# Reworking the projections and the first key pass of a two-layer gated cross-attention kernel

## The reference

```python
x = x + tanh(g_xattn[0]) * L0_xattn(layernorm(x), ctx, Wq, bq, Wkv, bkv, Wp, bp)
x = x + tanh(g_ffn[0])   * L0_ffn(layernorm(x), ...)          # mixture of low-rank experts
x = x + tanh(g_xattn[1]) * L1_xattn(layernorm(x), ctx, wq, bq, wkv, bkv, wp, bp)
x = x + tanh(g_ffn[1])   * L1_ffn(layernorm(x), ...)          # ternary weights

# L0_xattn: one softmax of every token over the keys of all 8 sequences
q = fq_sym((x @ Wq + bq) / 4, per token and head)             # round(q / s) * s, s = max|q| / 127
k = fq_sym(cond @ Wkv[:, :256] + bkv[:256], per key and head)
v = fq_sym(cond @ Wkv[:, 256:] + bkv[256:], per column, over all keys)
attn = fq_unsigned(softmax(q k^T), per row)                   # steps of max / 255
out = (attn @ v) @ Wp + bp

# L1_xattn: within a sequence
out = qdq(softmax(q k^T / 4) @ v) @ qdq(wp)^T + bp            # qdq: round(x / s) * s per row, s = max|x| / 127
```

## Time and profile before

| | us |
|---|---|
| median of three executions | 6873.82 |
| profiled execution | 6872.02 |
| its span | 6870.2 |
| first_keys, from its first POOL memset to the next stage | 122.16 to 552.89 |
| first_values | 552.89 to 703.03 |
| first_attention up to the first matmul | 703.03 to 732.82 |
| first row maxima, then the main loop | 732.82 to 5011.6 |
| project(0) | 5016.03 to 5081.78 |
| feed-forward, second queries and keys, second attention | to 6448 |
| project(1) | 6449.45 to 6550.16 |
| gated feed-forward | to 6870.2 |

### The profile page before, as it was taken

The page is one execution under the profiler, slowest core; times in us unless marked ns, Lnnn a source line. Parts: engine busy times, 40 slices in busy tenths (PEclk is TensorE's granted clock), DMA queues, the critical chain, the costliest instruction groups (busy, mean ns, idle before and its releaser), DMA issues. The chain is left out here.

```text
span 6870.2 us, 178673 instructions
## 1 busy us (share of the span) xinstructions
PE 5802.4 (84%) x63503; PEld 2380.6 (35%) x63510; DVE 5704.3 (83%) x8942; ACT 4387.7 (64%) x4251; POOL 3741.3 (54%) x3973
## 2 busy tenths in 40 slices
PE   2771699999999999999999999999949487999523
PEld 2331133333333333333333333333334353544311
DVE  5886699999999999999999999999943556777655
ACT  0330089988989889989889989989912013666301
POOL 2331078888888888878888888888810001000000
PEclk7995599999999999999999999999969697999756
DMA  1442211011011011011011011011020078877500
GB/s 57 112 108 94 46 22 18 9 26 19 9 26 19 9 26 18 10 26 18 10 26 18 11 25 19 11 25 19 10 48 0 19 303 181 116 112 114 85 28 9
DMA packets 182852, 319.86 MB, mean 47 GB/s; under 512 B 97220, under 2 KB 143813, under 8 KB 176803
## 3 DMA queue, kind: packets, MB, share of 16 engines
q1 hardware_dynamic: 181944, 307.93, 21.0%
HBM read 196.59 MB, written 113.33 MB: 45 GB/s over the span
## 5 line engine op out<-in xcount | busy, mean ns | idle before, releaser
L1024 DVE TENSOR_REDUCE a_mx<-PS 128x1 f32<-128x512 f32 x6620 | 4073.2, 688 | 230.1 <-PE PS L908 226.5
L995 ACT ACTIVATE a_e<-PS,a_sk 126x1024 f32<-126x1024 f32 x3264 | 3634.0, 1114 | 458.2 <-PE PS L893 109.6
L771 POOL TENSOR_SCALAR a_p<-a_e 126x1024 f16<-126x1024 f32 x3264 | 3418.1, 1047 | 641.0 <-ACT a_e L995 588.5
L908 PE MATMUL PS<-a_K,a_Q 48*128 48x512 bf16 (+1 forms) x6884 | 2109.8, 383 | 49.9 <-DMA a_K<-d_inv 49.9
L893 PE MATMUL PS<-a_Q,a_K 54*126 54x512 bf16 x6528 | 2113.3, 404 | 26.6 <-issue 17.4
L935 PE MATMUL PS<-a_e,a_sel 126*32 126x256 f32 x26112 | 1994.7, 382 | 0.0
L893 PEld LDWEIGHTS PS<-a_Q,a_K 54*126 54x126 bf16 x6528 | 615.4, 131 | 1377.3 <-issue 1319.6
L931 PE MATMUL PS<-a_p,a_V 128*32 128x256 f16 x13056 | 960.1, 284 | 14.1 <-ACT a_og L976 10.0
L931 PEld LDWEIGHTS PS<-a_p,a_V 128*32 128x32 f16 x13056 | 336.8, 93 | 1251.6 <-POOL a_p L771 1059.0
L935 PEld LDWEIGHTS PS<-a_e,a_sel 126*32 126x32 f32 x26112 | 756.1, 110 | 8.9 <-issue 2.4
L1891 DVE TENSOR_REDUCE b_mx<-PS 128x1 f32<-128x512 f32 x803 | 504.8, 685 | 188.4 <-PE PS L1775 188.4
(11 more groups left out here) (300 smaller groups left out, 3363.9 us busy)
## 6 DMA issues: line engine op xcount, KB each, us to landing
b_K<-d_k SPq DMA_DIRECT2D x210, 200.1 KB, 6.1
a_K<-d_k SPq DMA_DIRECT2D x102, 400.2 KB
d_v<-v1v SPq DMA_DIRECT2D x9, 3328.0 KB, 10.3
b_V<-d_v SPq DMA_DIRECT2D x36, 832.0 KB, 12.1
d_k<-k_T SPq DMA_DIRECT2D x400, 63.0 KB, 1.7
d_k<-k1p SPq DMA_DIRECT2D x54, 400.2 KB, 7.7
a_V<-d_v SPq DMA_DIRECT2D x68, 204.0 KB, 2.8
d_v<-vq SPq DMA_DIRECT2D x17, 803.2 KB
```

The costliest lines, as they stand in the source:

```text
L771: g.tensor_scalar(p[0:rows, kk % RE, :], e[0:rows, kk % RE, :], 1.0, SHIFT, ALU.mult, ALU.add).then_inc(rounded, 1)
L908: last = pe.matmul(self.PS[:, M_BANK + j % sh.SLOTS, c0:c0 + wd], Qb[M_ROWS, ii % 4, t * P:(t + 1) * P], Kb[M_ROWS, (ii // NC) % 2, k0:k0 ...
L995: a.activation(e[0:r, kk % RE, :], self.PS[0:r, e_bank(i, s):e_bank(i, s) + 2, :], ACT.Exp, scale=skb[0:r, hb, s:s + 1]).then_inc(exp_done, 1)
L1024: v.tensor_reduce(mx[:, col:col + 1], bank, AX.X, ALU.max).then_inc(max_done, 1)
```

## The change

- **first_keys.** Keys and values of both tiles now lie in a bank each. The bias is added by PE: DVE splits it once into three bf16 parts (rows 0, 32 and 64 of `bp`), and a 96-row bf16 matmul with a matrix of ones in those rows (`pick`) adds it to each of the four PSUM regions. DVE reads the keys straight from PSUM; ACT makes the values (`v_raw`) and their magnitudes (`v_abs`), and casts the high and middle bf16 parts. DVE keeps a running maximum of the magnitudes (`v_top`). DVE works on group g and the rest of group g - 1 in turn; PE turns group g - 2; ACT evacuates group g - 3 in two copies of 1008 columns and one of 252. SP stores a group with three DMAs.
- **first_values.** The maximum over partitions is taken by two PE transposes, a reduction of 2 x 126, two diagonal matrices and one matmul with ones. Scaling goes in two halves; each head's store and column sums are released as the head is rounded.
- **first_attention.** The three key parts for the row maxima are loaded first, in five pieces of keys, and PE waits for each piece where it needs it. POOL clears the 34 semaphores of the earlier stages ahead of its memsets.
- **project.** Sums are loaded as 16 rows, turned on PE, and their reciprocals taken from PSUM; no trip through DRAM. Layer 0: ACT spreads the reciprocals over each head's 16 columns, PE turns them, DVE applies them and the value scales in one instruction a half. Layer 1: the output is turned before the reciprocals are applied, bank by bank; rows and weight go as integers in bf16 through PE, the scales are applied to the product, the bias (times the gate) is added to x early. In both, DVE takes the product bank by bank while PE goes on.

```diff
@@ first_keys @@
+                self.link(v, v.tensor_copy(bp[:, :], bkv[:, :]), self.dv)
+                self.link(v, v.tensor_tensor(bt[:, 0, :], bkv[:, :], bp[:, :], ALU.subtract), self.dv)
+                self.link(v, v.tensor_copy(bm[:, :], bt[:, 0, :]), self.dv)
+                self.link(v, v.tensor_tensor(bt[:, 1, :], bt[:, 0, :], bm[:, :], ALU.subtract), self.dv)
+                v.tensor_copy(bp[32:64, :], bm[32:64, :]).then_inc(bias_ready, 1)
+                v.tensor_copy(bp[64:96, :], bt[64:96, 1, :]).then_inc(bias_ready, 1)
+                v.wait_ge(bias_ready, 2)
+                v.sem_inc(bias_ready, 1)
...
+                def scales(g):
...
+                        self.link(v, v.tensor_reduce(sc, by_head(ps), AX.X, ALU.max, apply_absolute_value=True), self.dv)
+                        self.link(v, v.tensor_scalar(sc, sc, 1.0 / 127.0, 1e-8, ALU.mult, ALU.max), self.dv)
+                        self.link(v, v.reciprocal(rc, sc), self.dv)
+                        if s.stop == GT:
+                            v.sem_inc(rk_ready, 1)
+                        self.link(v, v.tensor_tensor(by_head(tmp[0:n, b, s, :]), by_head(ps), along(rc, 3, HD), ALU.mult), self.dv)
+                    v.sem_inc(kv_seen, 1)
...
+                    b = g % 2
+                    v.wait_ge(cast, 2 * g + 1)
+                    for s, n in spans(g):
+                        self.link(v, v.tensor_tensor(tmp2[0:n, b, s, :], kf[0:n, b, s, :], parts[0:n, b, HI, s, :], ALU.subtract), self.dv)
+                    v.sem_inc(to_cast, 1)
...
+                def largest(g):
+                    v.wait_ge(v_taken, g + 1)
+                    for s, n in spans(g):
+                        top = self.v_top[0:n, s, :]
+                        self.link(v, v.tensor_tensor(top, v_abs[0:n, g % 2, s, :], top, ALU.max), self.dv)
...
+                    for s, n in spans(g):
+                        self.link(v, v.tensor_scalar(parts[0:n, b, INT, s, :], tmp[0:n, b, s, :], ROUND, ROUND, ALU.add, ALU.subtract), self.dv)
...
+                    v.wait_ge(cast, 2 * g + 2)
+                    for s, n in spans(g):
+                        self.link(v, v.tensor_tensor(parts[0:n, b, LO, s, :], tmp2[0:n, b, s, :], parts[0:n, b, MID, s, :], ALU.subtract), self.dv)
+                    v.sem_inc(parts_ready, 1)
...
+                        self.link(v, v.tensor_tensor(by_head(kf[0:n, b, s, :]), by_head(parts[0:n, b, INT, s, :]), along(sc, 3, HD), ALU.mult), self.dv)
+                    v.sem_inc(to_cast, 1)
...
+                for g in range(NG):
+                    scales(g)
+                    if g >= 1:
+                        rest(g - 1)
+                    whole(g)
+                    if g >= 1:
+                        last(g - 1)
+                    scaled(g)
+                    largest(g)
+                rest(NG - 1)
+                last(NG - 1)
@@ first_keys, PE and ACT @@
+                    for y in range(2):
+                        for j, n in tiles(g):
+                            kv = self.PS[0:n, 2 * (g % 2) + y, j * D:(j + 1) * D]
+                            for c in range(2):
+                                pe.matmul(kv, cT[:, g % RC, c, j * KT:j * KT + n], W[:, c, y * D:(y + 1) * D],
+                                          start=(c == 0), stop=False)
+                            last = pe.matmul(kv, pick[0:96, 0:n], bp[0:96, y * D:(y + 1) * D], start=False, stop=True)
...
+                def values(g):
+                    a.wait_ge(kv_ready, g + 1)
+                    if g >= 2:
...
+                        ps = self.PS[0:n, 2 * (g % 2) + 1, :].rearrange("p (t d) -> p t d", d=D)[:, s, :]
+                        a.activation(self.v_raw[0:n, g * GT + s.start:g * GT + s.stop, :], ps, ACT.Copy)
+                        ins = a.activation(v_abs[0:n, g % 2, s, :], ps, ACT.Abs)
+                    ins.then_inc(v_taken, 1)
...
+                    for i in range(2):
+                        a.activation(kT[:, g % 2, 2 * i:2 * i + 2, :, :].rearrange("p i c n -> p (i c n)"),
+                                     self.PS[:, 4 + i, :].bitcast(BF16)[:, 0:4 * GW], ACT.Copy).then_inc(self.ac, 1)
+                    a.activation(iT[:, g % 2, :], self.PS[0:HEADS * IROWS, 6, :].bitcast(BF16)[:, 0:GW], ACT.Copy).then_inc(self.ac, 1)
...
+                for g in range(NG):
+                    if g >= 3:
+                        evacuate(g - 3)
+                    if g >= 1:
+                        high(g - 1)
+                    values(g)
+                    if g >= 1:
+                        middle(g - 1)
+                evacuate(NG - 3)
+                high(NG - 1)
+                middle(NG - 1)
+                evacuate(NG - 2)
+                evacuate(NG - 1)
 
@@ first_values, DVE @@
+                L(v.tensor_tensor(self.v_top[:, 0, :], self.v_top[:, 0, :], self.v_top[:, 1, :], ALU.max))
+                v.sem_inc(top_ready, 1)
...
+                L(v.tensor_reduce(top[:, :], self.PS[:, 2, 0:2 * P].rearrange("p (c k) -> p c k", c=2)[:, :, 0:KT], AX.X, ALU.max))
+                for c in range(2):
+                    L(v.tensor_scalar(spread[:, c, :], self.idf[:, :], top[:, c:c + 1], None, ALU.mult))
+                v.sem_inc(spread_ready, 1)
...
                 for c in range(2):
+                    w = slice(c * P, (c + 1) * P)
+                    L(v.tensor_tensor(self.v_raw[:, :, w], self.v_raw[:, :, w], along(rv[:, w], 1, NKT), ALU.mult))
                     for h in range(8):
+                        if c == 1:
+                            v.wait_ge(stored, 16 * 9)
+                            v.wait_ge(summed, 1)
                         L(v.tensor_scalar(vq[:, h, :, 0:HD], self.v_raw[:, :, (8 * c + h) * HD:(8 * c + h + 1) * HD],
                                           ROUND, ROUND, ALU.add, ALU.subtract))
-                    v.sem_inc(half, 1)
+                        v.sem_inc(done, 1)
@@ first_attention, POOL and SP @@
+                for s in self.early_sems:
+                    g.sem_clear(s)
...
+                for i in range(FIRST):
+                    k0, k1 = i * sh.WHOLE // FIRST * BANK, (i + 1) * sh.WHOLE // FIRST * BANK if i < FIRST - 1 else sh.NK
+                    for row, part in M_KEYS:
+                        sp.dma_start(Kb[row:row + HD, 0, k0:k1], self.d_k0[part, 0, :, k0:k1]).then_inc(ld_first[i], 16)
                 load_scales(sp, 0, 0)
...
+                    sp.wait_ge(ld_first[i], FIRST_LOADED[i])
+                sp.sem_inc(ld_k[0], 16 * 3)
                 for at in range(V_DMAS):
@@ project, both layers @@
+                sp.dma_start(s[:, :], self.d_s[layer][0]).then_inc(ld_s, 16)
+                for c in range(2):
+                    sp.dma_start(o[:, c, :], o_src[:, c, :]).then_inc(ld_o, 16)
...
+                for t in range(NT):
+                    ins = pe.transpose(self.PS[:, 0, t * HEADS:(t + 1) * HEADS], s[:, t * P:(t + 1) * P], self.idf[0:HEADS, 0:HEADS])
...
+                v.wait_ge(s_turned, 1)
+                self.link(v, v.reciprocal(r[:, :, :].rearrange("p t h -> p (t h)"), self.PS[:, 0, 0:NT * HEADS]), self.dv)
...
@@ project, layer 0 @@
+                        a.wait_ge(r_ready, 1)
+                        for c in range(2):
+                            a.activation(rx[:, c, :, :].rearrange("p t (h d) -> p t h d", d=HD), along(r[:, :, 8 * c:8 * c + 8], 3, HD),
...
+                            self.link(v, v.scalar_tensor_tensor(out=o[:, c, :], in0=o[:, c, :], scalar=sv[:, c:c + 1],
+                                                                in1=self.PS[:, 4 * c:4 * c + 4, :].rearrange("p b n -> p (b n)"),
+                                                                op0=ALU.mult, op1=ALU.mult), self.dv)
...
+                            v.wait_ge(full, b + 1)
+                            self.link(v, v.tensor_tensor(y, self.PS[:, b, :].rearrange("p (t d) -> p t d", d=D), along(bp[:, :], 1, 2),
+                                                         ALU.add), self.dv)
+                            self.link(v, v.scalar_tensor_tensor(out=xs, in0=y, scalar=self.gates[:, layer:layer + 1], in1=xs,
+                                                                op0=ALU.mult, op1=ALU.add), self.dv)
@@ project, layer 1 @@
+                    turn_sums(pe)
+                    self.turn_int_weight(pe, wi, sw, 1, 2)
+                    pe.wait_ge(ld_o, 32)
+                    pe.wait_ge(r_ready, 1)
+                    pe.wait_ge(self.weight_taken, self.weights)
...
+                    v.wait_ge(ld_w, 32)
+                    self.int_weight(v, W, wi, wT, sw, st, self.gates[:, layer:layer + 1], 1, 2)
+                    self.link(v, v.tensor_scalar(bp[:, :], bp[:, :], self.gates[:, layer:layer + 1], None, ALU.mult), self.dv)
+                    self.link(v, v.tensor_tensor(self.x[:, :, :], self.x[:, :, :], along(bp[:, :], 1, NT), ALU.add), self.dv)
+                    reciprocals(v)
...
```

(32 more changed lines are left out.)

395 lines of the change are left out of this document (224 added, 171 removed).

## The result

The changed kernel takes 6694.3 us (median of four runs, 6692.3 to 6695.5); the kernel before takes 6871.6 on the same chip (four runs, 6865.4 to 6882.4). The ratio is 0.974, 95% interval 0.9723 to 0.9757. The prediction was 6689, range 6650 to 6735: right, 5 us off. The span of the profiled execution went from 6870.2 to 6692.8 us, 177.4 less.

| stage | before | after | difference | predicted |
|---|---|---|---|---|
| up to the start of first_keys | 122.2 | 121.0 | -1.2 | 0 |
| first_keys | 430.7 | 372.8 | -57.9 | -46.8 |
| first_values | 150.1 | 100.1 | -50.0 | -50.8 |
| first_attention, to its first matmul | 29.8 | 10.3 | -19.5 | -19.5 |
| to TensorE's restart behind the first row maxima | 131.3 | 124.3 | **-7.0** | 0 |

The account below looks back on a forecast made before the run. PE bounds the unedited main loop, DVE's serial chain first_keys, latency the projections. Savings of 46.8 (first_keys), 50.8 (first_values), 19.5 (first_attention's start), 27.4 and 40.3 (projections) total 184.8 us off 6872.0; adjusted to the median, 6689, range 6650 to 6735.

## What to carry to other kernels

Look at what an engine idles for at each jump of a hardware loop, and once more after an edit of anything ahead of the loop: instructions added far away can cost or return a microsecond-sized stall for each trip, and a burst of loads issued at the jump makes it longer. Shift the loop with a few idle instructions where the engine waits anyway, and check every later loop too, since they all move. Where a long memset of GpSimd and a short one-input SBUF instruction of VectorE meet, let VectorE's start first: here it was 0.61 us against 19.33.

## What the runs showed that was not expected

- The first attention's loop jump costs TensorE 2.5 to 3.4 us at best; with the next block wanted 1.5 us later, 8.0 to 8.9 in all in the kernel after, of which some 3 are the fetch behind 400 KB of loads.
- From the restart until some 5 us behind the double stall the granted clock is 0.50, the level of 1.2 GHz; behind the single stall of the kernel before it is back sooner (0.71 over 1902.2 to 1908, 1.00 from there). Yet the stretch grew by 31.8 us, no more than the stalls' 32.8. The window in the kernel after:

```profile
1771.00:1782.00 11.00, 6.67 (x48) 1.72 (x46) 3.87 (x6) 3.18 (x3) 2.09 (x2) 0.50 0.03 4
```

- Two VectorE multiplications of 128 elements took 19.33 us beside a memset of GpSimd that had begun first, and 0.61 ahead of it.
- 39 increments of TensorE vanished in a wait of 10 us; 217 did not, and the first matmul came 23.4 us later, 33.8 us into the stage: some 0.15 us each, by estimate, where the expectation had 0.06.
